# Where two attention layers join: the second group's weights scaled and rounded on ScalarE, the first keys' and values' weights split earlier, low rotated parts earlier, and the fills in another order

## The reference, cut to what matters

```python
x = _layernorm(x + _L0_attn_ref(x, Wq, bq, Wk, bk, Wv, bv, Wo, bo))   # 32 heads of 16, causal
x = _layernorm(x + _L0_xattn_ref(x, ctx, ctx, mask, wq, wk, wv, wo))  # 32 query heads, 8 key/value heads of 128
x = _layernorm(x + _L0_ffn_ref(x, 4-bit weights with scales and zeros))
...
# _L0_xattn_ref
q = _rope((query @ wq).reshape(bs, s, 32, 128).transpose(0, 2, 1, 3))
k = _rope((key @ wk).reshape(bs, s, 8, 128).transpose(0, 2, 1, 3))
v = (value @ wv).reshape(bs, s, 8, 128).transpose(0, 2, 1, 3)
scores = jnp.einsum('bhgqd,bhkd->bhgqk', qg, k) / scale     # 4 query heads share one key head
w = jax.nn.softmax(jnp.where(mask, scores, -1e9), axis=-1)
out = jnp.einsum('bhgqk,bhkd->bhgqd', w, v) ... @ wo
```

## Time and profile before

| what | value |
|---|---|
| median of the three runs | 884.78 us |
| span of the profiled execution, first to last instruction | 882.2 us |
| the profiled execution's own time | not listed apart; the median is 2.6 us over the span |
| mean granted TensorE clock | 0.991 |
| PE busy in the span | 842.7 us (96%) |
| VectorE, GpSimd, ScalarE busy | 718.1, 601.9, 497.2 us |

### The profile page before, as it was taken

One profiled execution on the slowest core, in us unless ns is written; L12 is line 12 of the kernel. 1 busy time (PEld: TensorE's weight loads), 2 busy tenths in 40 slices (PEclk: granted clock), 3 DMA queues, 4 the chain that ended last, 5 costly groups with the idle time before them and its releaser, 6 DMA issues.

```text
span 882.2 us, 17330 instructions
## 1 busy us (share of the span) xinstructions
PE 842.7 (96%) x6141; PEld 471.2 (53%) x6141; DVE 718.1 (81%) x1121; ACT 497.2 (56%) x1487; POOL 601.9 (68%) x534
## 2 busy tenths in 40 slices
PE   9899999999899999999999999999999799999997
PEld 4667777655455555554555555555555444333443
DVE  5598898887787888699788788797899564899897
ACT  5788888543555555565565565555555552777400
POOL 1265959896666776677677567578888542887895
PEclk9999999999999999999999999999999899999999
DMA  6765245103124412414225125124431322230011
GB/s 178 231 208 171 64 148 162 53 17 104 37 78 139 108 37 73 108 38 133 56 33 150 38 44 148 25 55 114 85 91 25 90 41 74 90 121 18 1 48 48
DMA packets 119893, 76.75 MB, mean 87 GB/s; under 512 B 72861, under 2 KB 104064, under 8 KB 119808
## 3 DMA queue, kind: packets, MB, share of 16 engines
q1 hardware_dynamic: 117504, 74.99, 31.6%
q10 hardware_dynamic: 2304, 0.66, 0.3%
HBM read 52.50 MB, written 6.36 MB: 67 GB/s over the span
## 4 chain that ended last, share of the span: by engine, by line
PE 47%; POOL 18%; DVE 14%; ACT 9%; issue 8%; DMA 4%; SPq 0%; ACTq 0%; POOLq 0%; DVEq 0%
PE bank L361 13%; PE bank L362 12%; PE bank L363 12%; POOL rot L640 3%; ACT prob L957 2%; DVE total L1316 2%; ACT prob L817 2%; POOL q2l L646 2%; POOL pn L657 2%; DVE rsin L1180 1%; POOL xqs L589 1%; POOL deq L669 1%; POOL xql L593 1%; POOL left L673 1%; DMA pT<-pn 1%
## 5 line engine op out<-in xcount | busy, mean ns | idle before, releaser
L650 POOL TENSOR_TENSOR prob<-prob,rden 128x512 f32<-128x512 f32 x64 | 66.6, 1041 | 129.1 <-DVE rden L1245 129.1
L640 POOL TENSOR_TENSOR rot<-rcos,rsin 128x512 f32<-128x512 f32 x80 | 106.6, 1333 | 14.3 <-DVE rsin L1180 14.2
L361 PE MATMUL bank<-aTh,xqh 128*128 128x512 f16 x256 | 97.0, 379 | 2.1 <-DVE aTl L1070 1.1
L361 PE MATMUL bank<-xoh,o2h 128*128 128x512 f16 x256 | 97.8, 382 | 0.0
L362 PE MATMUL bank<-xol,o2h 128*128 128x512 f16 x256 | 97.8, 382 | 0.0
L363 PE MATMUL bank<-xoh,o2l 128*128 128x512 f16 x256 | 97.6, 381 | 0.0
L363 PE MATMUL bank<-aTh,xql 128*128 128x512 f16 x256 | 97.0, 379 | 0.0
L362 PE MATMUL bank<-aTl,xqh 128*128 128x512 f16 x256 | 97.0, 379 | 0.0
L957 ACT ACTIVATE prob<-bank,ebias 128x128 f32<-128x128 f32 x256 | 90.6, 366 | 2.1
L1180 DVE SCALAR_TENSOR_TENSOR rsin<-bank,sinq 64x512 f32<-64x512 f32 x128 | 88.1, 688 | 1.7
L646 POOL TENSOR_TENSOR q2l<-rot,q2h 128x512 f16<-128x512 f32 x64 | 82.2, 1285 | 4.4 <-ACT q2h L853 4.4
(11 more groups left out here) (215 smaller groups left out, 2632.7 us busy)
## 6 DMA issues: line engine op xcount, KB each, us to landing
tst<-tables SPq DMA_DIRECT2D x11, 768.0 KB, 5.7
xqs<-in_xwq SPq DMA_DIRECT2D x8, 1024.0 KB, 7.0
xos<-in_xwo SPq DMA_DIRECT2D x8, 1024.0 KB, 5.7
qst<-in_fq SPq DMA_DIRECT2D x11, 384.0 KB, 3.5
kstk<-stack SPq DMA_DIRECT2D x48, 64.0 KB, 2.3
qstk<-stack SPq DMA_DIRECT2D x21, 128.0 KB, 2.6
xs<-in_ctxT SPq DMA_DIRECT2D x2, 1024.0 KB, 7.7
res<-in_x SPq DMA_DIRECT2D x1, 2048.0 KB, 8.7
```

The costliest lines, as they stand in the source:

```text
L361: pe.matmul(out_ap, ah, bh, start=first, stop=False)
L640: nc.gpsimd.tensor_tensor(rot[:, r % 2, :], rcos[:, r % 2, :], rsin[:, r % 2, :], ALU.add).then_inc(rope_rot, 1)
L650: nc.gpsimd.tensor_tensor(prob[:, v % 2, :].rearrange("p (h k) -> p h k", h=QH), prob[:, v % 2, :].rearrange("p (h k) -> p h k", h=QH), rd ...
```

## The change: what it does

It has six parts.

1. `HELPED_QKV` = group 1 of `xq`, `xk`, `xv` and `HELPED_OUT` = pieces 2 and 3 of `xo`'s group 0, eight pieces in all: ScalarE makes the high part and then scales the float32 buffer in place (`help_piece`, two activations); GpSimd waits for that (`help_scaled`) and does the subtraction alone (`helped_lo`).
2. `KV_FIRST`: the keys' and values' pieces of the groups 0 and 1 come before the queries'; group 0's at steps 36 and 37 and its queries' at 41 to 44, group 1's at 53 and 54 and its queries' at 55 to 58. `xo`'s group 0 is split at 45, 50, 61, 62. On SP's queue `load_kv(0)` and `load_q(0)` go ahead of `bring_keys(5)`, `load_kv(1)` ahead of `load_q(1)`, and `load_o(1)` and `load_kv(2)` are moved. PE waits for the piece that a fill needs, not for all six.
3. In steps before T0, GpSimd does the low rotated part before the step's piece, not after it.
4. In the steps T0 and T0 + 1, VectorE takes over both "o" fills before `row_sum_inverse`. At T0, ScalarE does the exponentials before the last cast of the joint.
5. Fills of the steps T0 + 2 to T0 + 4: "k" of block 2 behind the turns of the batches 4 and 5, the turn of batch 7 one step later. Group 1 of `xo` is split one step later.
6. At v = 4 `merge(1)` is done before the two "q" fills of that step.

```diff
-    plan += [(T0 + 2, "k", (2,)), (T0 + 2, "t", (0, 4)), (T0 + 2, "t", (0, 5)), (T0 + 3, "t", (0, 6)), (T0 + 3, "t", (0, 7))]
+    plan += [(T0 + 2, "t", (0, 4)), (T0 + 2, "t", (0, 5)), (T0 + 2, "k", (2,)), (T0 + 3, "t", (0, 6)), (T0 + 4, "t", (0, 7))]
...
+HELPED_QKV, HELPED_OUT = (1,), (2, 3)
+KV_FIRST = (4, 5, 0, 1, 2, 3)
...
             stack_rows(4)
-            stack_rows(5)
-            load_q(0)
-            load_kv(0)
+            stack_rows(5, ((load_kv, 0), (load_q, 0)))
             stack_rows(6)
             sp.wait_ge(tab_out, 32)
             load_o(0)
+            load_kv(1)
             load_q(1)
             stack_rows(7)
-            load_kv(1)
-            load_o(1)
...
+            def helped_lo(hi, lo, src, lo_done):
+                nonlocal helps_done
+                helps_done += 1
+                pool.wait_ge(help_scaled, helps_done)
+                nc.gpsimd.tensor_tensor(lo, src, hi, ALU.subtract).then_inc(lo_done, 1)
...
                 inverse_sds(0, t - 1)
+                if t < T0:
+                    for f in fills_at(t - 1):
+                        if f in ROPES:
+                            rotated_lo(f)
                 pieces(t)
...
+            def help_piece(hi, src):
+                split_hi(hi, src, E_W)
+                split_hi(src, src, E_W).then_inc(help_scaled, 1)
...
-                rotations(fills_at(t - 1)[:1])
+                if v > 0:
+                    rotations(fills_at(t - 1)[:1])
                 bank_splits(turned_first(t))
                 if v < STEPS:
                     exps(v)
-                rotations(fills_at(t - 1)[1:])
+                rotations(fills_at(t - 1)[1:] if v > 0 else fills_at(t - 1))
...
                 early = [f for f in fills_at(t)[:1] if f in ROPES] + turned_first(t)
+                early += [f for f in fills_at(t) if FILLS[f][1] == "o"]
...
-                    if f == first_fill(g):
+                    if g in POOL_QKV:
+                        pe.wait_ge(xq_lo, 6 * g + 1 + KV_FIRST.index({"k": 4, "v": 5, "q": 3}[kind]))
+                    elif f == first_fill(g):
                         pe.wait_ge(xq_lo, 6 * (g + 1))
...
+                if v == 4:
+                    merge(v - 3)
                 for f in fills_at(t)[1:]:
                     fill(f)
-                if 3 <= v <= STEPS + 2 and v != STEPS + 1:
+                if 3 <= v <= STEPS + 2 and v not in (4, STEPS + 1):
                     merge(v - 3)
```

More of the change, by code:

```diff
@@ L322, in decoder_kernel @@
         w1_hi, w1_lo = sem("w1_hi"), sem("w1_lo")
+        help_scaled = sem("help_scaled")
         piece_scaled, piece_hi = sem("piece_scaled"), sem("piece_hi")
@@ L369, in rope_out, with qkv_tiles @@
             return q2h[:, what[0] % 2, what[1], :], q2l[:, what[0] % 2, what[1], :]
+        def qkv_tiles(g, piece):
+            if piece < 4:
+                return xqh[:, g % 2, piece, :], xql[:, g % 2, piece, :], xqs[:, piece, :]
+            hi, lo, src = ((xkh, xkl, xks), (xvh, xvl, xvs))[piece - 4]
+            return hi[:, g % 2, :, :], lo[:, g % 2, :, :], src[:, :, :]
         def block_cols(n):
@@ L423, in bring_keys, with stack_rows @@
                                      ).then_inc(stack_in[j % 2], 16)
-            def stack_rows(j):
+            def stack_rows(j, loads=()):
                 keep_rows(j, 0, k1_out, 2 * j - 1)
                 keep_rows(j, 2, q1_out, 2 * j)
+                for load, g in loads:
+                    load(g)
                 if j >= 2:
@@ L538, in _ @@
                     turn_probabilities(t - T0 - 1)
-                for g in range(2, G):
-                    if QKV_SLOT[g - 1][3] + 1 == t:
+                for g in range(1, G):
+                    if g > 1 and QKV_SLOT[g - 1][3] + 1 == t:
                         load_q(g)
-                    if QKV_SLOT[g - 1][5] + 1 == t:
+                    if g > 1 and QKV_SLOT[g - 1][3 if g == 2 else 5] + 1 == t:
                         load_kv(g)
@@ L626, in pieces @@
                 for g in POOL_QKV:
-                    for piece in range(6):
+                    for piece in KV_FIRST:
                         if QKV_SLOT[g][piece] == t:
@@ L727, in _ @@
                 for f in fills_at(t - 1)[:1]:
-                    if f in ROPES:
+                    if f in ROPES and v >= 0:
                         rotated_lo(f)
@@ L838, in qkv_hi, with help_qkv, help_out @@
                 split_hi(dst, src, E_W).then_inc(xq_hi, 1)
+            def help_piece(hi, src):
+                split_hi(hi, src, E_W)
+                split_hi(src, src, E_W).then_inc(help_scaled, 1)
+            def help_qkv(g, piece):
+                if piece == KV_FIRST[0]:
+                    act.wait_ge(v1_psum, BLOCKS)
+                    act.wait_ge(xkv_in, 32 * (g + 1))
+                if piece == 0:
+                    act.wait_ge(xq_in, 16 * (g + 1))
+                hi, _, src = qkv_tiles(g, piece)
+                help_piece(hi, src)
+            def help_out(g, h):
+                act.wait_ge(xo_in, 16 * (g + 1))
+                help_piece(xoh[:, g % 2, h, :], xos[:, h, :])
             def o_weight_hi(g, h):
@@ L872, in weight_pieces @@
             def weight_pieces(t):
+                for g in HELPED_QKV:
+                    for piece in KV_FIRST:
+                        if QKV_SLOT[g][piece] == t:
+                            help_qkv(g, piece)
+                for g in POOL_OUT:
+                    for h in HELPED_OUT:
+                        if OUT_SLOT[g][h] == t:
+                            help_out(g, h)
                 for g in range(len(POOL_QKV), G):
@@ L1415, in _ @@
                 for f in fills_at(t)[1:]:
-                    consume(f)
+                    if f not in early:
+                        consume(f)
                 if t in LATE_TURN:
```

35 lines of the change are left out of this document (22 added, 13 removed).

## The result

The changed kernel takes 896.91 us (median of 4 runs, 891.94 to 899.5), the kernel before 884.73 in the same comparison (883.44 to 885.17): a ratio of 1.014, 95% interval 1.0123 to 1.0156. It is slower by 12.2 us, where 885.8 was forecast, with 888.6 as the upper end of the range.

The account below looks back on a forecast made before the run. PE was taken as the bound behind the joint, and GpSimd as the cause of PE's first-half gaps in it. 882.2 - 0.4 + 1.3 = 883.1, 885.7 with what lies around it; given as 885.8, range 880.4 to 888.6.

Parts of the forecast that it names:

- The ring is no faster: Steps before T0: cast, exponentials, ScalarE's pair, GpSimd's subtraction and sum take 5.9 us a turn, against 5.73 before.
- The waits of 1.23 and 1.66 us: First half, PE: these waits go; new ones of about 2.3 and 0.2 us come at tile 63's turn; gain 0.4.
- The norm of batch 0: First half: norm at 161.6 in place of 162.22, so that PE gains 0.6 us there.
- given back at step 57: ScalarE's pair holds `v2h` until about 175.8, so step 59's "q" fill stays at 178.50 and the 0.6 us is lost.
- The clock in the first half: Half clock behind tile 63's wait: no term in the prediction, which counted lost clock in the second half only, 1.15 us.
- I cost them at nothing ... the loss is up to 1.5 us: Earlier loads ahead of `bring_keys(5)`: no cost, rows wanted 8 us later at step 40; without that cover, up to 1.5 us.
- 1.5 + 3.5 + 0.9 + 0.5 + 1.15 = 7.5: Second half, us lost: `p_lo(0)`'s DMA, "k" fill, `merge(1)`, "q" fill, half clock; 6.2 before.
- The waits for `merge(1)` and the q fill: Second half: PE waits 0.9 us at `merge(1)`, and the "q" fill 0.5 us for batch 7's `aTl`.
- rival 1: GpSimd was the pace and is relieved: the first half's 4.75 us of waits go; 881.3, or 880.0; chance 0.2.
- -0.4 and +1.3: The sum's two terms: first half 0.4 us faster, second half 1.3 us slower.
- Rival 2: VectorE gets faster: eight norms at 0.54 us in place of 0.93, 3.1 us at most; 884.3; chance 0.12.
- Rival 3: Slower outright: second half's "k" fill starts later than forecast, with a longer clock fall; loads add; 888; chance 0.17.

Follow-up runs that it names:

- a_ring: a_help with GpSimd's rotation sum ahead of its subtraction of a helped piece in the steps from 59 to T0 - 1: 886.91 us.
- a_help: Changed kernel with the loads back, the first group's pieces where they stood, and the second half of the kernel before: 889.98 us.
- b_loads_kv: Kernel before, with the first group's loads ahead of the sixth block's stacked rows, keys' and values' load before the queries': 890.07 us.
- after_q: Changed kernel with the queries' load ahead of the keys' and values' load: 892.30 us.
- b_loads: Kernel before, with the first group's loads ahead of the sixth block's stacked rows, queries' load first: 885.99 us.
- f_four: a_help with helped subtractions a step later behind rotation sums, ScalarE's bank splits ahead of its pair, and the first two output pieces helped too: 879.77 us.
- b_second: Kernel before, with the second half of the change alone, weights still scaled and rounded by GpSimd: +4.4 us, ratio 1.0048.
- a_loads_back: Changed kernel with only its first group's loads back behind the sixth block's keys, that group's pieces one to three slots later: 894.17 us.

## Why the prediction was wrong

Its steps, in its order, by the starts of the changed kernel:

- **"The ring is no faster"**: right. The waits of 1.23 and 1.66 us went and the two new ones came as written, 0.18 and 2.29 us (0.2 and about 2.3), and a_ring removed them by breaking the ring alone. At tile 63's turn PE is 0.42 us ahead, measured from step 52 (54.00 against 54.42), 0.4 predicted. The pair took 1.17 us from its first start to its second's end (197.31 to 198.48), 1.13 taken.
- **The norm of batch 0** came 0.49 us sooner (0.6), **given back at step 57**: the q fill stands at 29.44 us behind step 52, 29.42 before. Right for this kernel. But it held only since GpSimd had no backlog at step 52, thanks to the earlier pieces of the first group: without them a_help takes 4.5 us more than before from step 52 to T0.
- **The clock in the first half** was not in the sum: behind the wait of 2.29 us it fell, and 1.45 us went. I let the clock fall for the second half's wait only.
- **"I cost them at nothing ... the loss is up to 1.5 us"** is the step that failed most: 5.8 us by the first column, a wait of 4.3 by starts and about 1.5 for the clock behind it. The 8 us of cover were not there. Counted from the landing of the last row, the slack was 2.2 us; the rows' issue then came 2.1 us later and the last of them took 6.9 us to land in place of 2.5. Together 6.5, less 2.2: 4.3. b_loads_kv shows that this loss is the loads' alone, after_q that 4.6 of it, by the medians, are their order's.
- **"1.5 + 3.5 + 0.9 + 0.5 + 1.15 = 7.5"** was 11.3 by starts. The mechanism was right: `p_lo(0)`'s DMA 1.84 (1.5), the k fill 4.11 (3.5), the clock behind it 1.46 (1.15). The waits for `merge(1)` and the q fill did not come. In their place, unseen: `weigh(2)` 2.21 us and a second fall of the clock, 1.68. GpSimd's timeline after has `rot` of the late k ahead of the low part that `weigh(2)`'s DMA takes:

```profile
249.40 1.26 POOL L664 TENSOR_TENSOR rot<-rcos,rsin 128x512 f32<-128x512 f32 x1 [5.28 <-DVE rsin L1234]
250.62 1.16 POOL L681 TENSOR_TENSOR pn<-prob,pn 128x512 f16<-128x512 f32 x1
```

A slip changed nothing: the range's lower end, 880.4, is called rival 1's, which is 880.0.

In sum: predicted -0.4 and +1.3; the columns say +5.76 for the loads, +1.03, +5.16, and +0.85 behind T0 + 5, of which 0.8 lie at the end of the attentions. There PE waits 4 us for `v2l` in both kernels and goes on at 692.08 and 704.13; the clock stands at half until 696.4 before and until 710.1 after, so PE works 4.35 and 6.0 us in it and loses half of the difference. The forecast had no such term.

One habit of the sum was wrong in both kernels: it adds a lost clock to the waits behind it. The kernel before lost 1.4 us of clock by this count, b_loads kept its clock in the same stage, and yet the two stages are 37.75 and 37.37 us, since the q fill then waits 1.62 us in place of 0.73.

**The rivals.** Rival 1 (GpSimd relieved) holds only once no inverse and no sum stands behind a helped subtraction, and two more pieces are helped: f_four is that kernel, and it gains 3.9 us from step 52 to T0. Rival 2: four norms of the first half did fall to 0.54 us, off the path; those beside `p_lo` stayed slow. Rival 3 had the sign and the place, and named the loads as an addition, at a quarter of their price.

Of the parts, the medians add up: a_help +5.9, b_second +4.4 and b_loads +1.9 are 12.2, the changed kernel's 12.2. This is partly chance, since the order of the loads costs 3.7 more and their early pieces give 3.6 back from step 52 to T0 (a_loads_back against after_q, 71.15 and 67.51 us).

## What to carry to other kernels

When work is split between two engines, put the half that waits for the other engine last in its queue, or a step later: here the same help cost 5.9 us with GpSimd's subtraction in line ahead of inverses and sums, and gained 4.7 with it behind them and GpSimd's other pieces off it too. Before a load is moved ahead of a small transfer, compare what the small one's issue and landing will lose with the time between its landing and its use (2.2 us here), not with the load's distance to its use. And price a new wait of PE of 2 us or so with the stretch at half clock that may follow: 1.5 to 1.7 us at each of the changed kernel's four, 2.8 in b_loads_kv. Leave that price out where PE would soon wait for another engine anyway.
